# Window scan and shifted-window attention: packed last channels, the input a chunk sooner, the order of the norms' steps

## What is computed

```python
def _ln(x, w, b): ...                      # layer norm over the 192 channels
def _mamba(xw, A, Bm, Cm):                 # along the 49 tokens of a 7x7 window
    xB = xw @ Bm
    def step(h, xb):
        h = xb + h @ A
        return (h, h)
    ...
    return h @ Cm
w = _ln(windows(_gn(x)), ln1_w, ln1_b)
w = _mamba(w, A, Bm, Cm)
y = _ln(w, ln2_w, ln2_b)
y = gelu(y @ W1 + b1) @ W2 + b2
x = x + w + y                              # first block
x = x + attention(_gn(x))                  # second: 7x7 windows shifted by 3, 12 heads
```

## Time and profile before

| | |
|---|---|
| median of 3 runs | 4776.58 us (4773.7 to 4777.52) |
| profiled execution | 4771.56 us, span 4769.8 us, mean granted clock 0.99 |
| TensorE busy | 4471.3 us (94%) |
| VectorE busy | 4085.7 us (86%) |
| ScalarE busy | 2351.8 us (49%) |
| GpSimd busy | 2642.9 us (55%) |
| 98 loads of `xt` | 384 KB each, 3.4 us from issue to landing |

### The profile page before, as it was taken

One profiled execution on the slowest core, in us unless ns is written; L12 is line 12 of the kernel. 1 busy time (PEld: TensorE's weight loads), 2 busy tenths in 40 slices (PEclk: granted clock), 3 DMA queues, 4 the chain that ended last, 5 costly groups with the idle time before them and its releaser, 6 DMA issues. The chain is left out here.

```text
span 4769.8 us, 122473 instructions
## 1 busy us (share of the span) xinstructions
PE 4471.3 (94%) x42440; PEld 3822.0 (80%) x42440; DVE 4085.7 (86%) x7841; ACT 2351.8 (49%) x4594; POOL 2642.9 (55%) x1714
## 2 busy tenths in 40 slices
PE   0599999999999999999969999999999999999998
PEld 0488888888888888888857888888888888888887
DVE  6798888888888888888838888888888888888887
ACT  0244444444444444444415555555555555555555
POOL 1245555455545554555536666666666666666665
PEclk9999999999999999999969999999999999999999
DMA  8011111111111111111112222222222222222222
GB/s 341 21 38 38 39 39 41 37 39 39 41 37 39 39 41 38 38 39 39 37 46 79 80 78 79 81 81 77 80 79 81 77 81 78 82 80 78 79 81 65
DMA packets 398996, 310.66 MB, mean 65 GB/s; under 512 B 140011, under 2 KB 397243, under 8 KB 397755
## 3 DMA queue, kind: packets, MB, share of 16 engines
q1 hardware_dynamic: 396212, 307.89, 21.9%
q10 hardware_dynamic: 2736, 2.14, 0.1%
HBM read 145.48 MB, written 87.33 MB: 49 GB/s over the span
## 5 line engine op out<-in xcount | busy, mean ns | idle before, releaser
L885 POOL TENSOR_TENSOR E<-E,ri 128x588 f32<-128x588 f32 x512 | 802.8, 1568 | 781.5 <-DVE ri L1092 781.5
L604 PE MATMUL ps_o<-w,g_hi 128*128 128x384 f32 x2352 | 709.7, 365 | 5.9 <-DVE g_lo L544 4.1
L416 ACT ACTIVATE gF<-ps_g,b1f 128x512 f32<-128x512 f32 x588 | 404.6, 688 | 392.8 <-PE ps_g L635 390.7
L604 PE MATMUL ps_o<-w,g_lo 128*128 128x192 f32 x2352 | 534.5, 254 | 0.0
L969 ACT ACTIVATE PT<-ps_t 98x588 f32<-98x588 f32 x512 | 338.9, 662 | 395.6 <-PE ps_t L1216 395.6
L1082 DVE SCALAR_TENSOR_TENSOR L<-ps_s,bias 128x588 f32<-128x588 f32 x512 | 394.6, 771 | 152.3 <-PE ps_s L1208 144.2
L1216 PE MATMUL ps_t<-ident,E 128*98 128x128 f32 x3072 | 441.8, 280 | 78.5 <-POOL E L885 78.4
L443 POOL TENSOR_TENSOR res<-xt,b2b 128x768 f32<-128x768 f32 x98 | 181.0, 1847 | 591.1 <-DVE x L492 591.1
L1216 PEld LDWEIGHTS ps_t<-ident,E 128*98 128x98 f32 x3072 | 313.8, 128 | 233.4 <-POOL E L885 198.1
L402 ACT ACTIVATE h_hi<-ps_h,hbias 128x512 fp32r<-128x512 f32 x196 | 123.1, 679 | 703.6 <-PE ps_h L619 703.6
L1208 PE MATMUL ps_s<-Kp,Q 64*64 64x196 f32 x6144 | 455.1, 342 | 2.7 <-DMA Kp<-K 2.7
(11 more groups left out here) (203 smaller groups left out, 12238.8 us busy)
## 6 DMA issues: line engine op xcount, KB each, us to landing
xs<-in_x SPq DMA_DIRECT2D x8, 4704.0 KB, 22.3
xt<-in_x SPq DMA_DIRECT2D x98, 384.0 KB, 3.4
x_cells<-x SPq DMA_DIRECT2D x784, 48.0 KB
xb<-x_cells SPq DMA_DIRECT2D x128, 294.0 KB
Vx<-V SPq DMA_DIRECT2D x512, 73.5 KB
out<-yo SPq DMA_DIRECT2D x128, 294.0 KB
Kp<-K SPq DMA_DIRECT2D x512, 49.0 KB, 1.8
gnr<-gn_rows SPq DMA_DIRECT2D x128, 192.0 KB
```

Of the source, the lines that this page charges most:

```text
L416: act.activation(gF[f % 4][:, :], ps_g[:, f % 2, :], ACT.Gelu, bias=b1f[:, f:f + 1]).then_inc(s_gelu, 1)
L604: last = pe.matmul(dst, g[:, f, P * k:P * (k + 1)], w, start=(f == 0 and i == 0), stop=(f == FT - 1 and i == 1))
L885: pool.tensor_tensor(e, e, ri[p][:, :].unsqueeze(2).to_broadcast([P, HEADS, T]), ALU.mult)\
```

## The change

- The weights of the scan's products (`wB`, `wA`) get 64 more columns: the lower parts of the output channels 128 to 191 beside the upper ones. One matmul with 128 output rows gives both products for these channels: six matmuls where there were ten. The lower rows of `ps_h` are copied to `h_low` by ScalarE, VectorE adds them (`h_b`), and the splits of h take the last channels from `h_b`.
- The input of chunk n+3 is loaded in slot n (before: n+2), once `res` of chunk n+1 is through, and ahead of the stores; the stores' own wait on `x1` goes, since the load's wait implies it.
- VectorE's group norm is one chunk ahead (`normed`, chunk n+3) and lies between `g_lo` f=1 and f=4, where the norm of `xn` was. The statistics of the first layer norm (`measured`, chunk n+3) lie at the end of VectorE's slot, behind the first half of `x1`.
- GpSimd takes the pow for `rsa` behind that for `rsb`, and a product for the offset after each (`ofa`, `ofb`).
- Both layer norms are applied by ScalarE as `rs * x + of`: `xn` (chunk n+2) at the start of its slot, ahead of `h_low`, `h_hi` and `y_hi`; `yb` (chunk n+1) at its end.
- In the attention stage one bias operand is another column of the same table.

```diff
+            def lower(self, t):
+                return self.parts[2 * t + 1][:, :]
+            def lower_beside(self, t):
+                return self.parts[2 * t][:, self.cols:self.cols + self.beside]
+            def packed_terms(self, data_hi, data_lo):
+                both = slice(self.cols - self.beside, self.cols + self.beside)
+                a_hi, _, b_hi, _ = self.parts
+                return ((a_hi[:, both], data_hi[:, 0, :]), (a_hi[:, both], data_lo[:, :]), (b_hi[:, both], data_hi[:, 1, :]))
...
             M1 = sb("M1", [P, NT, C])
-            W_B, W_A, W_C = (Split(ctx, name, C) for name in ("wB", "wA", "wC"))
+            W_B, W_A = (Split(ctx, name, C, CB) for name in ("wB", "wA"))
...
                 def slot(t, c):
...
                     n = CHUNKS * t + c
-                    if there(n + 2):
-                        upto(sp, s_res, n + 1)
-                        sp.dma_start(xt[c][:, :, :],
-                                     x[TPC * c:TPC * (c + 1), :, bass.ds(t + 1, 1), :]
-                                     .rearrange("k p t c -> p k (t c)")).then_inc(s_x[c], 16)
...
+                    if there(n + 3):
+                        upto(sp, s_res, n + 2)
+                        load(t + 1 + c, 1 - c)
                     if there(n - 1):
...
-                        sp.wait_ge(s_x1, n)
+                        if isinstance(n, int):
+                            sp.wait_ge(s_x1, n)
...
+                load(0, 0)
                 slots(sp, slot)
...
+                    if there(n + 2):
+                        act.wait_ge(s_of1, n + 3)
+                        for k in range(TPC):
+                            last = act.activation(xn[c][:, k, :], xn[c][:, k, :], ACT.Identity,
+                                                  bias=ofa[:, k:k + 1], scale=rsa[:, k:k + 1])
+                        last.then_inc(s_xn, 1)
                     if there(n + 1):
                         d = 1 - c
                         act.wait_ge(s_scan, n + 2)
                         upto(act, s_cm, n)
-                        for k, rows in enumerate((P, CB)):
-                            last = act.activation(h_hi[d][0:rows, k, :], ps_h[0:rows, k, :], ACT.Identity,
-                                                  bias=hbias[0:rows, k:k + 1])
-                        last.then_inc(s_hh, 1)
+                        act.activation(h_low[0:CB, :], ps_h[CB:P, 1, :], ACT.Copy).then_inc(s_hc, 1)
+                        act.activation(h_hi[d][:, 0, :], ps_h[:, 0, :], ACT.Identity, bias=hbias[:, 0:1])
                     if there(n):
                         act.wait_ge(s_t2, n + 1)
                         upper_parts(y_hi, ps_g).then_inc(s_yh, 1)
+                    if there(n + 1):
+                        act.wait_ge(s_hb, n + 2)
+                        act.activation(h_hi[d][0:CB, 1, :], h_b[0:CB, :], ACT.Copy).then_inc(s_hh, 1)
                     if there(n):
...
+                    if there(n + 1):
+                        act.wait_ge(s_of2, n + 2)
+                        act.wait_ge(s_rsum, n + 2)
+                        upto(act, s_t2, n + 1)
+                        for k in range(TPC):
+                            last = act.activation(yb[:, k, :], tok_tile(ps_r, k), ACT.Identity,
+                                                  bias=ofb[:, k:k + 1], scale=rsb[:, k:k + 1])
+                        last.then_inc(s_y, 1)
...
+                def root(m):
+                    pool.wait_ge(s_ve1, m + 1)
+                    upto(pool, s_xn, m)
+                    pool.tensor_tensor(rsa[:, :], vea[:, :], neg_half[:, :], ALU.pow).then_inc(s_rs1, 1)
+                    pool.wait_ge(s_rs1, m + 1)
+                    pool.tensor_tensor(ofa[:, :], nma[:, :], rsa[:, :], ALU.mult).then_inc(s_of1, 1)
...
-                    if there(n + 2):
-                        pool.wait_ge(s_ve1, n + 3)
-                        pool.tensor_tensor(rsa[:, :], vea[:, :], neg_half[:, :], ALU.pow).then_inc(s_rs1, 1)
...
+                        pool.wait_ge(s_rs2, n + 2)
+                        pool.tensor_tensor(ofb[:, :], nmb[:, :], rsb[:, :], ALU.mult).then_inc(s_of2, 1)
+                    if there(n + 3):
+                        root(n + 3)
...
+                root(0)
                 slots(pool, slot)
...
+                def measured(m, t, c):
+                    dve.wait_ge(s_gn, m + 1)
+                    for k in range(TPC):
+                        last = dve.bn_stats(s6a[:, k, :], xn[c][:, k, :])
+                    last.then_inc(s_st1, 1)
+                    dve.wait_ge(s_w, 16 * WEIGHT_LOADS)
+                    dve.wait_ge(s_st1, m + 1)
+                    for k in range(TPC):
+                        last = dve.bn_aggr(mva[:, k, :], s6a[:, k, :])
+                    last.then_inc(s_ag1, 1)
+                    dve.wait_ge(s_ag1, m + 1)
+                    upto(dve, s_of1, m)
+                    dve.tensor_scalar(nma[:, :], mva[:, :, 0], -1.0, None, ALU.mult)
+                    dve.tensor_scalar(vea[:, :], mva[:, :, 1], LN_EPS, None, ALU.add).then_inc(s_ve1, 1)
                 def slot(t, c):
                     n = CHUNKS * t + c
-                    if there(n + 2):
-                        dve.wait_ge(s_x[c], 16 * (t + 2))
-                        upto(dve, s_t1, n + 1)
-                        r = slice(TPC * c, TPC * (c + 1))
-                        dve.tensor_tensor(xn[c][:, :, :], xt[c][:, :, :], R1[:, r, :], ALU.mult).then_inc(s_gs, 1)
-                        dve.wait_ge(s_gs, n + 3)
-                        dve.tensor_tensor(xn[c][:, :, :], xn[c][:, :, :], M1[:, r, :],
-                                          ALU.subtract).then_inc(s_gn, 1)
                     if there(n + 1):
-                        dve.wait_ge(s_hh, n + 2)
-                        lower_parts(h_hi[1 - c], h_lo[1 - c], ps_h, hbias).then_inc(s_hl, 1)
+                        d = 1 - c
+                        dve.wait_ge(s_hc, n + 2)
+                        dve.scalar_tensor_tensor(out=h_b[0:CB, :], in0=ps_h[0:CB, 1, :], scalar=hbias[0:CB, 1:2],
+                                                 in1=h_low[0:CB, :], op0=ALU.add, op1=ALU.add).then_inc(s_hb, 1)
                     if there(n):
...
@@ -513,30 +577,21 @@
                         dve.wait_ge(s_w2, n)
                         x1_half(1 - c, 1, s_xb, n).then_inc(s_x1, 1)
-                    if there(n + 2):
-                        dve.wait_ge(s_gn, n + 3)
-                        for k in range(TPC):
-                            last = dve.bn_stats(s6a[:, k, :], xn[c][:, k, :])
-                        last.then_inc(s_st1, 1)
-                        dve.wait_ge(s_w, 16 * WEIGHT_LOADS)
-                        dve.wait_ge(s_st1, n + 3)
-                        for k in range(TPC):
-                            last = dve.bn_aggr(mva[:, k, :], s6a[:, k, :])
-                        last.then_inc(s_ag1, 1)
-                        dve.wait_ge(s_ag1, n + 3)
-                        dve.tensor_scalar(vea[:, :], mva[:, :, 1], LN_EPS, None, ALU.add).then_inc(s_ve1, 1)
+                    if there(n + 1):
+                        d = 1 - c
+                        dve.wait_ge(s_hh, n + 2)
+                        dve.scalar_tensor_tensor(out=h_lo[d][:, :], in0=ps_h[:, 0, :], scalar=hbias[:, 0:1],
+                                                 in1=h_hi[d][:, 0, :], op0=ALU.add, op1=ALU.subtract)
+                        dve.tensor_tensor(h_hi[d][CB:P, 1, :], h_b[0:CB, :], h_hi[d][0:CB, 1, :],
+                                          ALU.subtract).then_inc(s_hl, 1)
                     if there(n):
                         for f in LO_DVE[:2]:
                             dve.wait_ge(s_gh, FT * n + f + 1)
                             dve.tensor_tensor(g_lo[:, f, :], gF[f % 4][:, :], g_hi[:, f, :], ALU.subtract)\
                                 .then_inc(s_gld, 1)
-                    if there(n + 2):
-                        dve.wait_ge(s_rs1, n + 3)
-                        for k in range(TPC):
-                            last = dve.tensor_scalar(xn[c][:, k, :], xn[c][:, k, :], mva[:, k, 0:1], rsa[:, k:k + 1],
-                                                     ALU.subtract, ALU.mult)
-                        last.then_inc(s_xn, 1)
+                    if there(n + 3):
+                        normed(n + 3, t + 1 + c, 1 - c)
                     if there(n):
                         for f in LO_DVE[2:]:
@@ -555,6 +610,7 @@
                             last = dve.bn_aggr(mvb[:, k, :], s6b[:, k, :])
                         last.then_inc(s_ag2, 1)
                         dve.wait_ge(s_ag2, n + 2)
+                        dve.tensor_scalar(nmb[:, :], mvb[:, :, 0], -1.0, None, ALU.mult)
                         dve.tensor_scalar(veb[:, :], mvb[:, :, 1], LN_EPS, None, ALU.add).then_inc(s_ve2, 1)
                     if there(n + 2):
                         dve.wait_ge(s_xh, n + 3)
@@ -563,12 +619,6 @@
                         d = 1 - c
```

(33 more changed lines are left out.)

44 lines of the change are left out of this document (28 added, 16 removed).

## The result

The kernel after the change takes 5089.5 us in the median (5085.9 to 5091.0), the kernel before on the same chip 4777.1: a ratio of 1.0654, 95% interval 1.0636 to 1.0673. The forecast was 5012, slower by 235; it is slower by 312.

The account below looks back on a forecast made before the run. TensorE, 99.9% busy in the scan, was taken as the bound at 22.79 us a chunk; after, 10.2 + 15.17 = 25.4, +2.6 a chunk: +247 over about 95 chunks, -3 for the others, giving 5012 us (4860 to 5090).

Parts of the forecast that it names:

- The packed matmuls: Scan's matmuls, from their start T: ten become six, 0.92 us less per chunk; hidden layer's start W possible at T+7.97.
- The new chain: From T (scan's matmuls start) to W (hidden layer's): statistics, pow, `ofa`, four activations, splits put W at T+10.2, TensorE idling 2.2.
- one bias less and an overlap: ScalarE's `h_low`, `h_hi` and two of `y_hi`: before 2.22 us for the four, now a little less, ending at T+8.7.
- The covered work: ScalarE's later `h_hi` and `yb`, VectorE's `h_b` and `h_lo`: ready before TensorE wants them, cost nothing; uncovered, `yb` costs 1.85.
- The group norm in the gap: VectorE between `g_lo` f=1 and f=4: load and GpSimd delay it, second layer at W+11.65 for W+10.2, next T at W+15.17.
- the wait before L659: Sign: TensorE waits for `g_lo` before the second layer's matmuls (L604 in the kernel before), 1.5 us a chunk.
- the lock's cost: VectorE operations with two SBUF operands wait for GpSimd's running `g_lo`; half of this cost is 0.5 us a chunk.
- the second wait: TensorE's second layer waits for `g_lo`, held by load and lock: W+11.65 in place of W+10.2.
- the clock: Rival: TensorE's clock falls to the 1.2 GHz level in the new gaps, +2 us a chunk, 5200 us; 6%.
- the chain is hidden: Rival: `h_low` starts by T+4.4, W at T+7.97, 21.5 us a chunk, 4651; with the lock's stall 4800; 6%.
- the load and the lock are free: Rival: input load and lock cost nothing, only the chain ahead of y does: 23.8 us a chunk, 4870 us; 13%.
- A packed form that is no cheaper: Rival: the six full-width matmuls of the scan save nothing, +88 us on top; 2%.

Follow-up runs that it names:

- experiment 5: Three runs: packing undone in the changed kernel, 5014.3 us; packing alone in the kernel before, 4816.2; packing undone with `xn` activations and group norm both moved, 4726.8.
- packed_only: The kernel before with the packed matmuls alone, VectorE's two subtractions for h behind its x1 sums; 4816.2 us.
- late_short_lo: The changed kernel with ScalarE's `xn` activations behind the splits of h and y, and GpSimd's two `g_lo` cut to 4 of 512 columns; 4693.9 us.
- gap_filled: The changed kernel with 12 unused transposes of the identity on TensorE, in the gap before the hidden layer's matmuls; 5030.2 us.
- norms_late: The changed kernel with ScalarE's four `xn` activations moved behind the splits of h and y; 4792.9 us.
- both_unpacked: The changed kernel with `xn` activations behind the splits of h and y, group norm's two operations on GpSimd, and the packing undone (20 matmuls); 4726.8 us.
- pool_norm: The changed kernel with the group norm's product and subtraction moved from VectorE to GpSimd, behind its two `g_lo` and VectorE's last; 5051.2 us.
- unpacked: The changed kernel with the packing alone undone: 20 matmuls for the scan's product, no `h_low` and `h_b`; 5014.3 us.
- pool_norm_filled: The changed kernel with the group norm's two operations on GpSimd and 12 filling transposes on TensorE; 4914.1 us.

## Why the prediction was right, and where it was not

**The packed matmuls.** Right in size: 16 matmuls 0.23 apart, 0.90 us a chunk where TensorE is full (experiment 5), and W at T+7.98 without the chain. Right too that nothing of it arrives here. What I didn't see is that it does harm here: it widens the gap, and `h_low` in the place of an `h_hi` makes ScalarE's chain 0.2 us longer, by overlaps that are missing before and behind it. Why they are missing was not tried.

**The new chain.** Predicted T+10.2, measured 10.40; the 0.2 are 19 us of the 77 that are missing. By its links, in the chunk shown:

| link ends | predicted, after T | measured |
|---|---|---|
| `vea` | 3.41 | 3.34 |
| pow | 4.51 | 4.51 |
| `ofa` | 4.75 | 4.79 |
| four activations | 6.66 | 6.68 |
| `y_hi`, upper parts | 8.7 | 8.98 |
| `y_lo` and `y_hi`, lower parts | 10.15 | 10.40 |
| W | 10.2 | 10.45 |

The two prices that no row of before had are right: the product on four elements 0.20 (taken 0.2, bounds 0 and 1.02), the activation with two per-partition operands 0.537 (taken 0.53). The error arose in one term, the four activations of h and y behind the `xn` norms ("one bias less and an overlap"), put at 2.04 and measured at 2.30. The formula of the Trainium skill that was weighed there (page "ScalarE: Activation LUTs", section "What ACT_TABLE_LOAD costs") gave 532 ns and 1.85 for four; the trace agrees, with 537 and 1.86.

**The covered work.** Right: no wait list names `yb`, `h_lo` or the stores ahead of TensorE. The cover was needed, though: `h_hi<-h_b,h_hi` takes 1.80 us beside GpSimd's `res`, and packed_only shows the price when VectorE has no room.

**The group norm in the gap.** Right, link by link, in the chunks that keep the clock, a third of them; after W: load issued 3.25 (3.19), landed 6.5 (6.9), product done 8.37 (8.3), subtraction 10.34 (10.2), `g_lo` 11.54 (11.5), L659 11.67 (11.65), next T 15.21 (15.17). Of the signs that it named, the wait before L659 is 1.34 in these chunks (1.5) and 0.68 in the others, and TensorE's busy share is 88% (85%). The prediction called the lock's cost the weakest step. In these chunks its order was the one assumed, and the second wait is 1.6 in all (in the slowed ones the order is another, as shown above); late_short_lo measures the lock's part at 1.05, in a surrounding where the load lands 0.7 later. The rule of the Trainium skill (page "SBUF — State Buffer", section "Who interferes with whom") was that of two such instructions the first to issue blocks the other. By that rule, the trace agrees: the subtraction ends 0.81 after GpSimd's `g_lo` pair (1018.21 against 1017.40), much as `xn<-xt,R` did in the earlier trace rows, and with the partner cut short it takes its bare 0.96.

**What failed: the clock.** It stood as a rival with 6%, by itself, as "once a chunk that is +2 us: 5200". It came on top of the forecast and at a third of that price. In 64 of 97 chunks TensorE loses 1.6, and 0.92 are left after the cover of the second wait, 0.61 a chunk or 58 us; gap_filled measures 59.3. The step that failed is the treatment as an alternative: the gap that should lower the clock was a part of the likeliest case. "No row shows such a gap" was true of the rows that were chosen, but not of the trace of before. Near the start of the scan it has gaps of 2.89 and 3.44 us that begin at a granted clock of 1.00, and within 1.3 us of the end of each it is at 0.50 (TensorE's timeline, and busy time by stretches, columns as in rows 1):

```profile
177.43 0.36 PE L646 MATMUL ps_r<-wC_a_hi,h_hi 128*128 128x192 f32 x1 [2.89 <-DVE h_hi L482]
...
198.21 0.50 PE L635 MATMUL ps_g<-y_hi,w_a_hi 128*128 128x512 f32 x1 [3.44 <-DVE y_hi L480]
```

```profile
178.80:183.00 4.20, 3.43 (x16) 3.08 (x16) 2.93 (x16) 0.00 (x0) 1.02 (x1) 0.50 0.01 2
...
199.20:202.50 3.30, 3.30 (x9) 2.55 (x9) 0.68 (x6) 1.07 (x2) 1.02 (x1) 0.50 0.00 0
```

Both are longer than 2.2 us and don't settle its case, but they are nearer to it than 4.05, and each was followed by the low clock. With them in sight there was no ground for counting the clock at nothing.

**The sum, and luck.** The two errors, 19 for the chain and 58 for the clock, make 77 us, which is the distance from 5012 to 5089, but that they match so well is luck. The forecast's own sum gives 5015 on the profiled execution and about 5020 on the median, and nothing in it leads down to 5012. From 5020 the two errors would lead to 5097; the medians differ by 312, some 9 less than the steps of the profiled executions add up to (321), and so the time is 5089.5. That it lies inside the range is luck too: the upper end, 5090, stood for `ofa` at 1.0 us, which took 0.20, and it was the clock that used up the room. The mechanism of the two waits was right; the range held by 0.5 us.

**The rivals.** That the chain is hidden would have given 4800 with the second wait left; norms_late, which hides it by another order, gives 4793. That the load and the lock are free, 4870, is refuted by the rows above. A packed form that is no cheaper is refuted by both_unpacked.

## What to carry to other kernels

Before work is moved to an engine that is half idle, look where in its queue it lands: the four activations cost 297 us ahead of the chain (59 of them by way of the clock) against a place behind it, with the same instructions. Two operations of VectorE with two operands in SBUF were free on GpSimd, behind its own work, and cost 1.6 us a chunk in a gap of VectorE that GpSimd's work shares. Where a change must leave TensorE a gap of some 2 us, price the clock with it, and try to fill the gap: here 12 useless transposes were worth 59 us.

## What the runs showed of the hardware

- Gaps of 2.2 to 2.3 us once a chunk, with TensorE full around them but for the short wait before L659, lowered its clock to the 1.2 GHz level in two chunks of three, for 3.4 us each time. Near 1000 us the chunks come in turn: low from 0.2 us after W, low from 1.1 us after W, not low. The gap's length doesn't tell which: 2.29 before 1007.87 was spared and 2.19 before 1033.42 was not. Gaps of 2.4 to 2.6 in pool_norm gave 3.4 us in 61 chunks, 6.8 us in 24, and nothing in 10. Gaps of 0.9 to 1.4 in gap_filled, unpacked and pool_norm_filled, and of 1.3 to 1.6 in norms_late, left it at 1.00. What lies between 1.6 and 2.2 was not tried.
- Where both engines want the lock, they take turns. GpSimd's second `g_lo` of the chunk shown first (its timeline) took 2.01 in place of 1.27:

```profile
1015.38 2.01 POOL L500 TENSOR_TENSOR g_lo<-gF,g_hi 128x512 fp32r<-128x512 f32 x1
```

  VectorE's product came between the two and ended at 1016.24; the subtraction came after the second.
- The load of 384 KB took 3.3 us from issue to landing, 3.4 in the earlier trace rows. Issued a chunk sooner, it was still late by 0.56 us in late_short_lo, since it is issued when its buffer comes free and that moment follows from GpSimd's `res`.
